# A graph network on one core: the scatter of left-over sums split by tile and set between the gathers

## The chip, the cores and the metric

The kernel runs on 1 core of a Trainium2 chip. Its time is the device time of one execution in microseconds. The kernel before was run three times: 4803.33, 4816.18 and 4818.72 us, median 4816.18. One further execution was recorded by the hardware profiler; the profile and all rows below are of that one.

## The reference

The program is four layers of a message passing network (PNA) over 6250 nodes with 64 features and 206,250 directed edges. In a layer each node takes, over its incoming edges, the sum, the mean, the greatest, the least, the variance and the standard deviation of the messages:

```python
msg = jnp.concatenate([h[src], h[dst]], axis=1) @ WM + bM
s = jax.ops.segment_sum(msg, dst, num_segments=n)
mean_sq = jax.ops.segment_sum(msg * msg, dst, num_segments=n) / denom
mx = jax.ops.segment_max(msg, dst, num_segments=n)
mn = jax.ops.segment_min(msg, dst, num_segments=n)
agg = jnp.concatenate([mean, mx, mn, std, var, s], axis=1)
hu = jnp.concatenate([h, agg, agg * amp, agg * att], axis=1) @ WU + bU
out = leaky_relu(batchnorm(hu / sqrt(n)) @ Wmix + bmix) + h
h = relu(batchnorm(out)) + h
```

The part of a message that comes from the source, `h[src] @ WM[:64]`, is a row of a table with one row per node (64 values, and their 64 squares). The part that comes from the target is the same for all edges of a node and is added afterwards. So what has to be gathered are rows of the table.

## The kernel before, in words

Before the four layers the kernel sorts the edges of each node. It puts at most one edge per node and block of 125 source nodes into a one-hot matrix (the dense part), and lists the edges that are left over (the second and further edges of a node from one block) in up to 64 columns. The nodes are ordered by how many left-over edges they have and stand in 50 tiles of 128 (`RT = TILES = 50`).

A layer has two parts.

The **dense part** (VectorE: `dense_part`, TensorE: `chunk`) runs over 13 chunks (`NCH`) of 482 nodes (`CH`), and in each over 50 steps, one per block: 650 steps a layer. A step is three matmuls at L1638 into one of five PSUM banks (`RING`), whose result VectorE folds into a running maximum (`greatest`, L1271; for the first two steps of a chunk a copy, L1269), and three matmuls at L1645 that sum up in one bank through the chunk, which ScalarE copies out at its end (L565). The matmuls of a step wait for VectorE to have read the bank (`g_used`); VectorE waits for `g_ready`, which TensorE raises with the third matmul. The one-hot matrix comes from DRAM on SyncE's queue (L448), five steps at a time, five such loads ahead; in layer 0 VectorE makes it (`compare`, L1287) from loaded node numbers (`RE<-vd`) and SyncE stores it.

Beside it, GpSimd fetches the **left-over rows**. `COL_GROUPS` is a fixed list of 166 groups. A group is one column of one to three neighbouring tiles, 457 such columns (`STATIC`) in all, each fetched by one indirect DMA of 128 rows (L808, a gather) into one of five ring places (`RING_G`). Before a group GpSimd waits for two things: that the group five before it has been added up (`joined`), and that the dense part has come within 12 steps (`AHEAD`) of the step at which the group is due (`g_ready`). The due steps are spread evenly from step 56 to step 580 (`COL_SPAN`). VectorE works a group in between the maxima, in three parts (L1324 and L1325 greatest and least, L1328 mask, L1333 add), into the sums `acc3` of 256 values per node in `accL`.

The first tiles have the most columns: tile 0 has 29, tile 1 has 17, tile 49 has 2. The list takes column 0 of all tiles, then column 1 and so on, with the single ones of tile 0 spread over it, so high tiles get their last column early and low tiles late.

When the last group is added up, GpSimd **scatters** the sums, which lie in the order of left-over edges, to the DRAM tensor `left` in the order of the nodes: 50 indirect DMAs of 128 rows of 1 KB (L836), one per tile. It waits until all have landed (`lf_sc`) and loads them back with ten plain DMAs (L841), which the second part of the layer reads. Two branches ahead of the scatter are for graphs that need more columns than planned: `rest` and `more`, which both are read at run time.

The **node part** (`node_part`) takes the dense results and the loaded left-over sums together (L1449 and on), multiplies by `WU` and `Wmix`, and normalizes.

What sets the order of the work is each engine's own program: the engines meet only at semaphores. GpSimd's program is written out in full for one layer (all 166 groups) in a loop over four.

## Time and profile before

| what | value |
|---|---|
| median of three runs | 4816.18 us |
| span of the profiled execution | 4821.6 us |
| mean granted clock of TensorE | 0.935 of full speed |
| TensorE busy | 3895.8 us (81%), 19240 matmuls |
| VectorE busy | 3426.7 us (71%) |
| GpSimd busy | 2229.1 us (46%) |
| ScalarE busy | 508.7 us (11%) |

The profile gives no other time of that execution than its span, from the first to the last instruction. Its first 390 us are the sorting of the edges; then come four layers of about 1100 us. Layers 1 to 3 are alike: layer 1's maxima run from 1532 to 2453 us, and GpSimd's gathers from 1582 to 2308 us; the scatters follow at 2319 us, and the node part at 2456 us. Layer 0 carries the making of the one-hot matrix too.

Times in the rows are microseconds from the start of the span, durations of single instructions in ns where marked so. PE is TensorE, DVE VectorE, ACT ScalarE, POOL GpSimd, SP SyncE. A busy time on GpSimd for a DMA is the time in which it makes the descriptors, not the transfer.

### The profile page before, as it was taken

How to read it: one execution, taken by the hardware profiler on the slowest of the kernel's cores; microseconds unless marked ns; L12 is line 12 of the kernel's file. 1: busy time of each engine (PE TensorE's matmuls, PEld its weight loads, DVE VectorE, ACT ScalarE, POOL GpSimd, SP SyncE). 2: the span in 40 equal slices, each digit the busy share in tenths (PEclk: the TensorE clock that was granted, in tenths of full speed). 3: DMA queues.
4: the chain of work that ended last, by engine and by line, in shares of the span. 5: the costliest groups of instructions: out<-in, count | busy, mean ns of one | idle time of the engine just before them, and what ended most of it. 6: DMA issues, size and time to landing. Idle time of an engine off the chain costs nothing.

```text
span 4821.6 us, 69713 instructions
## 1 busy us (share of the span) xinstructions
PE 3895.8 (81%) x19240; PEld 2004.6 (42%) x19240; DVE 3426.7 (71%) x7809; ACT 508.7 (11%) x1496; POOL 2229.1 (46%) x2241
## 2 busy tenths in 40 slices
PE   0165999998688999999587999999597999899586
PEld 0022444443265444444265444444265444444255
DVE  5795888898477777777377777777367677777466
ACT  4211000000034000000034000000024000000024
POOL 6204566666500566666500556666500466666600
PEclk9987999999799999999799999999799999999898
DMA  6005888888741444444531444444441444444450
GB/s 176 9 16 146 223 228 217 229 234 212 208 155 58 139 137 136 139 136 136 155 117 55 136 132 127 146 135 131 140 151 40 130 137 140 134 136 131 133 171 28
DMA packets 302954, 667.77 MB, mean 138 GB/s; under 512 B 82191, under 2 KB 180677, under 8 KB 302435
## 3 DMA queue, kind: packets, MB, share of 16 engines
q1 hardware_dynamic: 188676, 419.32, 29.7%
q0 software_dynamic: 81280, 191.65, 15.3%
q10 hardware_dynamic: 32732, 54.15, 3.4%
q14 instruction: 208, 1.70, 0.1%
q8 instruction: 58, 0.95, 0.1%
HBM read 517.17 MB, written 151.72 MB: 139 GB/s over the span
## 4 chain that ended last, share of the span: by engine, by line
PE 58%; another core or an unknown queue 19%; DVE 10%; issue 6%; ACT 2%; POOL 2%; DMA 1%; ACTq 1%; DVEq 0%; SPq 0%; POOLq 0%
PE bank L1638 27%; PE bank L1645 24%; PE bank L1722 3%; DVE scr L1271 2%; POOL accL L766 1%; PE bank L1710 1%; DVE RE L1082 1%; POOL accL L758 1%; DVE accL L1038 1%; DMA RE<-vd 1%; DVE accL L1039 1%; PE bank L1620 1%; PE bank L1694 0%; ACT scr L690 0%
## 5 line engine op out<-in xcount | busy, mean ns | idle before, releaser
L808 POOL DMA_INDIRECT rows<-table,lists x1828 | 1832.8, 1003 | 1269.8 <-issue 645.0
L1638 PE MATMUL bank<-RE,split 126*128 126x482 bf16 x7800 | 2061.8, 374 | 346.5 <-DVE scr L1271 268.4
L1271 DVE TENSOR_TENSOR scr<-scr,bank 128x482 f32<-128x482 f32 x2496 | 1594.6, 649 | 1026.5 <-PE bank L1638 615.0
L1645 PE MATMUL bank<-RE,split 125*128 125x482 bf16 x7800 | 2058.5, 373 | 143.1 <-ACT scr L565 122.7
L1638 PEld LDWEIGHTS bank<-RE,split 126*128 126x128 bf16 x7800 | 749.8, 98 | 1272.9 <-DVE scr L1271 348.5
L1645 PEld LDWEIGHTS bank<-RE,split 125*128 125x128 bf16 x7800 | 766.8, 98 | 1016.1 <-ACT scr L565 128.9
L565 ACT COPY scr<-bank 128x482 f32<-128x482 f32 x52 | 29.1, 560 | 3704.9 <-PE bank L1645 1772.1
L1333 DVE TENSOR_TENSOR accL<-accL,rows 128x384 f32<-128x384 f32 (+2 forms) x664 | 342.8, 516 | 0.0
L1328 DVE SCALAR_TENSOR_TENSOR rows<-CNT,rows 128x384 f32<-128x384 f32 (+2 forms) x664 | 342.6, 516 | 0.0
L793 POOL MEMSET accL<- 128x3328 f32 x4 | 11.5, 2871 | 682.5 <-DVE split L1260 681.5
L836 POOL DMA_INDIRECT left<-accL,lists x200 | 195.6, 978 | 110.5 <-issue 110.5
L1324 DVE TENSOR_TENSOR accL<-accL,rows 128x192 f32<-128x192 f32 (+2 forms) x664 | 221.0, 333 | 1.7 <-issue 1.0
L1325 DVE TENSOR_TENSOR accL<-accL,rows 128x192 f32<-128x192 f32 (+2 forms) x664 | 220.7, 332 | 0.0
L1722 PE MATMUL bank<-W,rows 128*125 128x192 f32 x624 | 126.5, 340 | 39.8 <-ACT scr L690 39.8
L772 POOL DMA_INDIRECT pos_d<-accL,nid x50 | 50.1, 1002 | 230.5 <-DVE nid L1163 215.5
L1287 DVE TENSOR_SCALAR RE<-RE,col 126x2410 bf16<-126x2410 bf16 x130 | 113.2, 871 | 28.2 <-DMA RE<-vd 26.5
L1722 PE MATMUL bank<-W,RE 128*125 128x192 f32 x576 | 113.1, 332 | 20.2 <-ACT scr L690 19.3
L1722 PEld LDWEIGHTS bank<-W,rows 128*125 128x125 f32 x624 | 101.8, 193 | 47.9 <-issue 38.1
L1269 DVE COPY scr<-bank 128x482 f32<-128x482 f32 x104 | 67.0, 655 | 59.3 <-remote 28.4
L1722 PEld LDWEIGHTS bank<-W,RE 128*125 128x125 f32 x576 | 90.7, 187 | 28.0 <-issue 25.1
L1449 DVE TENSOR_TENSOR rows<-bank,accL 125x256 f32<-125x256 f32 x100 | 42.6, 426 | 77.8 <-PE bank L1698 76.1
L1710 PE MATMUL bank<-ident,aggb 125*128 125x125 f32 x600 | 83.4, 276 | 4.8 <-DVE aggb L1469 4.8
(272 smaller groups left out, 2370.6 us busy)
## 6 DMA issues: line engine op xcount, KB each, us to landing
RE<-ohd SPq DMA_DIRECT2D x395, 593.1 KB
RE<-vd SPq DMA_DIRECT2D x130, 593.1 KB
ohd<-RE SPq DMA_DIRECT2D x130, 593.1 KB
rows<-table,lists POOLq DMA_INDIRECT x1828
dense_d<-scr ACTq DMA_DIRECT2D x104, 241.0 KB
accL<-left POOLq DMA_DIRECT2D x40, 625.0 KB, 19.3
split<-dense_d ACTq DMA_DIRECT2D x16, 750.0 KB, 8.6
table<-accL SPq DMA_DIRECT2D x36, 250.0 KB
```

The source lines that it names most:

```text
L808: nc.gpsimd.indirect_dma_start(ring[:, b * GC + k, :], None, table, bass.IndirectOffsetOnAxis(ap=lists[:, c:c + 1], axis=0)).then_inc(col_ ...
L836: nc.gpsimd.indirect_dma_start(left, bass.IndirectOffsetOnAxis(ap=lists[:, t * PAY + D:t * PAY + D + 1], axis=0), acc3[:, t, :], None).the ...
L1271: nc.vector.tensor_tensor(accM[k % 2], accM[k % 2], G[k % RING][:, 0:CH], ALU.max).then_inc(S["g_used"], 1)
L1287: nc.vector.tensor_scalar(BK[b][0:NP + 1, :], VB[g % 2][0:NP + 1, :], answers[0:NP + 1, :], None, ALU.is_equal).then_inc(S["cmp"], 1)
L1324: nc.vector.tensor_tensor(acc[:, :, 2 * D:3 * D], acc[:, :, 2 * D:3 * D], got[:, :, 0:D], ALU.max)
L1325: nc.vector.tensor_tensor(acc[:, :, 3 * D:4 * D], acc[:, :, 3 * D:4 * D], got[:, :, 0:D], ALU.min).then_inc(S["tops"], 1)
L1328: nc.vector.scalar_tensor_tensor(got, bcast(CNT[:, t:t + w].unsqueeze(2), [P, w, 2 * D]), float(r), got, ALU.is_gt, ALU.mult).then_inc(S[" ...
L1333: nc.vector.tensor_tensor(acc[:, :, 0:2 * D], acc[:, :, 0:2 * D], got, ALU.add).then_inc(S["joined"], 1)
L1638: ins = nc.tensor.matmul(G[k % RING][:, 0:CH], split[0:NP + 1, ORDER[k], q, 0:2 * D], columns_of(k, NP + 1), start=q == 0, stop=q == 2)
L1645: ins = nc.tensor.matmul(SB[:, 0:CH], split[0:NP, ORDER[k], q, D:3 * D], columns_of(k, NP), start=k == 0 and q == 0, stop=k == TILES - 1 a ...
L1710: ins = nc.tensor.transpose(FPS[(2 * j + a) % 3][:, c * NP:(c + 1) * NP], agg[j % 2][0:NP, a, 2 * c:2 * c + 2, :], id125)
L1722: nc.tensor.matmul(u, aggT[j % 2][a][:, c * NP:(c + 1) * NP], W[:, W_U + c * 192:W_U + (c + 1) * 192], start=a == 0 and c == 0, stop=False ...
```

## The change

Each tile's scatter is issued as soon as five groups (`RING_G`) have gone by since its last group, so that the `joined` wait ahead of the group vouches that its sums are complete. Behind the gathers of a group at most one tile is scattered. A tile under 25 (`HALF`) waits for `acc_ready` first, the semaphore by which ScalarE tells that it has cleared these sums. What is left after the last group is scattered at the end as before. In the two branches for larger graphs the whole scatter is done again with semaphores of its own, and VectorE waits there for the first one before it changes the sums.

```diff
+LAST_GROUP = [max((g for g, (_, t0, w) in enumerate(COL_GROUPS) if t0 <= t < t0 + w), default=-1) for t in range(RT)]
...
+                def scatter(t, signal):
+
+                    nc.gpsimd.indirect_dma_start(left, bass.IndirectOffsetOnAxis(ap=lists[:, t * PAY + D:t * PAY + D + 1], axis=0),
+                                                 acc3[:, t, :], None).then_inc(S[signal], 16)
+
+                to_scatter = sorted(range(RT), key=lambda t: LAST_GROUP[t])
                 for g, (r, t, w) in enumerate(COL_GROUPS):
...
+                    done = [t for t in to_scatter if LAST_GROUP[t] + RING_G <= g][:1]
+                    for t in done:
+                        if t < HALF:
+                            wait(pool, "acc_ready", l * 3 + 3)
+                        scatter(t, "lf_sc")
+                        to_scatter.remove(t)
                 wait(pool, "joined", (l + 1) * NG + RING_G)
+                for t in to_scatter:
+                    scatter(t, "lf_sc")
                 with pool.If(rest > 0):
...
+                    for t in range(RT):
+                        scatter(t, "lf_rest")
+                    wait(pool, "lf_rest", (l + 1) * (16 * RT))
                 with pool.If(more > 0):
...
-                    pool.sem_inc(S["passed"])
-
-                for t in range(RT):
-                    nc.gpsimd.indirect_dma_start(left, bass.IndirectOffsetOnAxis(ap=lists[:, t * PAY + D:t * PAY + D + 1], axis=0),
-                                                 acc3[:, t, :], None).then_inc(S["lf_sc"], 16)
+                    for t in range(RT):
+                        scatter(t, "lf_more")
+                    wait(pool, "lf_more", (l + 1) * (16 * RT))
+
                 wait(pool, "lf_sc", (l + 1) * (16 * RT))
...
             def further_rounds(l):
 
+                wait(dve, "lf_sc", (l + 1) * (16 * RT))
...
                     wait(dve, "joined", (l + 1) * NG + RING_G)
+                    wait(dve, "lf_sc", (l + 1) * (16 * RT))
```

By the list 44 of the 50 tiles find a group, and 6 remain for the end. The due steps of the groups behind which a scatter stands, in runs of neighbouring groups: 192 and 195; 303 to 310 (3 scatters); 359 to 366 (3); 403 to 420 (6); 445 to 456 (4); 480 to 497 (6); 511 to 527 (6); 538 to 552 (5); 558 to 580 (9).

GpSimd's program at the layer's end, before: the last three groups of gathers, and behind the branches the whole scatter in a row. L364 are the registers and waits.

```order
L808 DMA rows<-table,lists 128x128 [waits g_ready]
L808 DMA rows<-table,lists 128x128 x2
L364 REGISTER_ALU
L364 REGISTER_ALU [waits joined]
L808 DMA rows<-table,lists 128x128 [waits g_ready]
L808 DMA rows<-table,lists 128x128
L364 ISA
L811 COMPARE_AND_BRANCH [waits joined]
...
L836 DMA left<-accL,lists 6400x256 x50
L364 REGISTER_ALU
L841 DMA accL<-left 125x1280 [waits lf_sc]
L841 DMA accL<-left 125x1280 x9
```

The same place now: L818 are the gathers, L807 the scatters, L861 the loads.

```order
L818 DMA rows<-table,lists 128x128 [waits g_ready]
L818 DMA rows<-table,lists 128x128 x2
L807 DMA left<-accL,lists 6400x256 [waits acc_ready]
L367 REGISTER_ALU
L367 REGISTER_ALU [waits joined]
L818 DMA rows<-table,lists 128x128 [waits g_ready]
L818 DMA rows<-table,lists 128x128
L807 DMA left<-accL,lists 6400x256 [waits acc_ready]
L367 ISA
L807 DMA left<-accL,lists 6400x256 [waits joined]
L807 DMA left<-accL,lists 6400x256 x5
```

Six of the fifty scatters are left in the row; each group in front of it has one of its own.

In the stretch of groups due at steps 480 to 497, before:

```order
L808 DMA rows<-table,lists 128x128 x2
L364 REGISTER_ALU
L364 REGISTER_ALU [waits joined]
L808 DMA rows<-table,lists 128x128 [waits g_ready]
L808 DMA rows<-table,lists 128x128 x2
```

and now:

```order
L818 DMA rows<-table,lists 128x128 x2
L807 DMA left<-accL,lists 6400x256 [waits acc_ready]
L367 REGISTER_ALU
L367 REGISTER_ALU [waits joined]
L818 DMA rows<-table,lists 128x128 [waits g_ready]
L818 DMA rows<-table,lists 128x128 x2
L807 DMA left<-accL,lists 6400x256 [waits acc_ready]
```

A group of three gathers has become three gathers and a scatter.

## Rows read from the trace of the kernel before

**Rows 1.** The page's costliest groups: busy us, mean ns | idle before.

```profile
L808 POOL DMA_INDIRECT rows<-table,lists x1828 | 1832.8, 1003 | 1269.8 <-issue 645.0
...
L836 POOL DMA_INDIRECT left<-accL,lists x200 | 195.6, 978 | 110.5 <-issue 110.5
```

**Rows 2.** Windows of layer 1: from:to, length, busy us of each engine.

```profile
core 0: us, PE busy (x) PEld busy (x) DVE busy (x) ACT busy (x) POOL busy (x), PEclk, DMA share, GB/s
...
1596.00:2181.00 585.00, 537.51 (x2549) 246.75 (x2547) 435.04 (x958) 4.48 (x8) 365.60 (x371) 0.97 0.48 137
2181.00:2318.00 137.00, 131.08 (x615) 60.24 (x614) 108.84 (x245) 1.12 (x2) 78.28 (x80) 0.96 0.48 138
2318.00:2394.00 76.00, 27.63 (x113) 11.14 (x112) 12.58 (x20) 0.56 (x1) 53.95 (x60) 0.65 0.43 134
2394.00:2454.00 60.00, 59.41 (x287) 27.81 (x285) 31.60 (x49) 0.37 (x1) 0.00 (x0) 0.98 0.83 244
```

**Rows 3.** Timeline of VectorE: start, us busy, line, [idle before <-releaser].

```profile
2326.42 0.66 DVE L1271 TENSOR_TENSOR scr<-scr,bank 128x482 f32<-128x482 f32 x1 [0.57 <-DVE scr L1271]
...
2342.15 0.66 DVE L1271 TENSOR_TENSOR scr<-scr,bank 128x482 f32<-128x482 f32 x1 [5.68 <-remote]
2355.49 0.66 DVE L1271 TENSOR_TENSOR scr<-scr,bank 128x482 f32<-128x482 f32 x1 [12.68 <-remote]
2371.59 0.66 DVE L1271 TENSOR_TENSOR scr<-scr,bank 128x482 f32<-128x482 f32 x1 [15.45 <-remote]
...
2400.30 0.66 DVE L1271 TENSOR_TENSOR scr<-scr,bank 128x482 f32<-128x482 f32 x1 [0.57 <-PE bank L1638]
2401.53 0.66 DVE L1271 TENSOR_TENSOR scr<-scr,bank 128x482 f32<-128x482 f32 x1 [0.56 <-PE bank L1638]
```

**Rows 4.** Timeline of GpSimd, layer 1: first and last scatter of 50, first loads.

```profile
2319.42 1.00 POOL L836 DMA_INDIRECT left<-accL,lists  x1 [10.89 <-issue]
...
2382.06 0.97 POOL L836 DMA_INDIRECT left<-accL,lists  x1 [0.30 <-issue]
2385.08 5.26 POOL L841 DMA_DIRECT2D accL<-left  x10 [2.04 <-DMA left<-accL,lists]
```

**Rows 5.** Timeline of TensorE in the row of scatters.

```profile
2334.09 0.77 PE L1638 MATMUL bank<-RE,split 126*128 126x482 bf16 x3
...
2356.20 1.39 PE L1638 MATMUL bank<-RE,split 126*128 126x482 bf16 x3 [10.74 <-DVE scr L1271]
```

**Rows 6.** Timeline of GpSimd: a row of 9 gathers, a row of 12.

```profile
2112.48 0.98 POOL L808 DMA_INDIRECT rows<-table,lists  x1 [2.73 <-PE bank L1638]
...
2122.52 0.95 POOL L808 DMA_INDIRECT rows<-table,lists  x1 [0.30 <-issue]
2127.47 0.95 POOL L808 DMA_INDIRECT rows<-table,lists  x1 [4.00 <-PE bank L1638]
...
2161.62 0.98 POOL L808 DMA_INDIRECT rows<-table,lists  x1 [1.16 <-PE bank L1638]
...
2175.66 0.95 POOL L808 DMA_INDIRECT rows<-table,lists  x1 [0.31 <-issue]
2179.49 1.01 POOL L808 DMA_INDIRECT rows<-table,lists  x1 [2.88 <-remote]
```

**Rows 7.** Timeline of VectorE: the last late wait beside each of these rows.

```profile
2125.40 0.66 DVE L1271 TENSOR_TENSOR scr<-scr,bank 128x482 f32<-128x482 f32 x1 [1.48 <-PE bank L1638]
...
2178.76 0.66 DVE L1271 TENSOR_TENSOR scr<-scr,bank 128x482 f32<-128x482 f32 x1 [4.65 <-remote]
```

**Rows 8.** Windows, L1271 alone: from:to, length, VectorE busy (count), PEclk, DMA.

```profile
1234.00:1311.00 77.00, 13.98 (x23) 0.69 0.58 178
...
1596.00:2181.00 585.00, 260.03 (x407) 0.97 0.48 137
...
2318.00:2394.00 76.00, 10.70 (x17) 0.65 0.43 134
```

**Rows 9.** Timeline of VectorE in layer 0, behind the scatters.

```profile
1335.50 0.85 DVE L1287 TENSOR_SCALAR RE<-RE,col 126x2410 bf16<-126x2410 bf16 x1 [20.54 <-DMA RE<-vd]
```

**Rows 10.** The loads at L841 in layer 1 (2384 to 2460 us).

```profile
DMA to landing us min/median/max: 5.5/19.8/44.5
```

More of the change, by code:

```diff
@@ L339, in build @@
             "kb_done big_v big_ready big_next big_found big_rows big_added big_reset "
-            "gathered listed own_done paid idx_ready summed added tops masked joined lf_sc "
+            "gathered listed own_done paid idx_ready summed added tops masked joined lf_sc lf_rest lf_more "
             "t_ps t_used mq_ready sq_done x_ready agg_a agg_v at_ps at_ev u_ps scaled hu_done ht_ps hut_ev fin_v shift "
```

## The prediction

> **What bounds the kernel now.** The profiled execution has a span of 4821.6 us, 5.4 us (0.1%) above the median of the three runs, 4816.18. I read first the costliest groups of the page: GpSimd issues 1828 gathers and 200 scatters, that is 457 and 50 in each of four layers [rows 1]. Then the busy times by stretch, to see what TensorE does meanwhile. A layer's dense part is 650 steps. A step is three matmuls at L1638, three at L1645 and one maximum on VectorE (L1271; L1269 for two of the fifty in a chunk). With GpSimd silent TensorE is busy for 59.4 of 60 us [rows 2] and a step takes 1.23 us (the last two of [rows 3]): there the matmuls bound it. Beside the gathers TensorE is busy for 537.5 of 585 us, and in the 76 us in which the scatters run for only 27.6 [rows 2]. So the scatter row, though it is on an engine that nobody seems to need just then, is the worst stretch of the layer.
>
> The timeline of VectorE shows how. In the row of scatters, from 2319.4 to 2383.0 us [rows 4], VectorE has its usual waits until 2326.4; then one maximum waits 5.7 us, the next 12.7, the next 15.5 [rows 3]. TensorE had issued matmuls at L1638 five banks ahead, the last at 2334.09, and then waited for VectorE, so it is TensorE's signal that comes late; the signal back takes effect within 0.1 us of the maximum's end (2355.49 + 0.66, matmul at 2356.20 [rows 5]). The first six scatters do no harm and the others nearly stop the two engines. Gathers do the same in small: after 9 in a row GpSimd pauses 4.0 us and VectorE's late wait is 1.5 us; in a row of 12 that wait is 4.7 us [rows 6, 7]. I take it that what hurts is GpSimd issuing without a pause, of either kind, from about the seventh DMA on. The trace doesn't say why.
>
> **What goes.** In layer 1 the window 2318 to 2394 holds 17 maxima at L1271 and 2 copies at L1269, 19 steps [rows 8]; at 1.23 us they need 23.4 us, so 52.6 of 76 us are lost. Layers 2 and 3 show the same 17 in 76 us each. In layer 0 the window 1234 to 1311 holds 23 and 2, so 30.8 us of work in 77: 46.2 lost. Behind it VectorE waits 20.5 us for a load of node numbers [rows 9], which stays. In the changed kernel six scatters are left at the end, after a wait for the last sums. Six is as many as did no harm. So up to 3 x 52.6 + 46.2 = 204 us go.
>
> What comes next there is not late: the six scatters take 6 x 1.28 = 7.7 us, their landing 2.0 (GpSimd's wait before the loads of the sums [rows 4]), the loads at most 44.5 us (median 19.8) after issue [rows 10]: some 55 us after the last sum, and 66 steps at 1.23 us, 81 us, are left of the dense part. The loads already ran beside full-speed matmuls at 1.23 us a step, so I take nothing for them.
>
> **What comes.** 44 scatters a layer go between the gathers, 176 in all, each at the end of a group. By the plan's table 5 stand near steps 190 to 310, 13 from 359 to 456, and 26 from step 480 to 580, there behind nearly every group. The added wait for the cleared sums (tiles under 25) was met hundreds of steps before. The other two added waits are in branches that this graph doesn't take (the trace has no instruction of them), and cost nothing.
>
> A group of three gathers comes every 524/457 x 3 = 3.44 steps, 4.23 us at TensorE's own pace. GpSimd needs 3 x 1.255 = 3.77 us for it, and with a scatter 5.04. (1.255 is the distance of two gathers in a row, 1.278 of two scatters [rows 4, 6].) Before, GpSimd could run ahead to its limit (12 steps, or five groups) and pause, and in the pause TensorE's signals got through. With a scatter behind each group it is slower than TensorE, so it pauses only when TensorE stalls. The price of a scatter between gathers is not in the trace. Bounds from rows:
> - 0 us, if it fits into the pauses: in 2181 to 2318 us GpSimd issues 80 gathers, 100.4 us, and is idle for 36.6; 26 scatters take 33.2.
> - 0.8 us: 5.04 - 4.23, GpSimd never pausing.
> - 1.2 us: the same, with the 2.9 us pause of the row of twelve behind every 12 to 15 DMAs, 0.2 us on each of the four: 5.04 + 0.9 = 5.9 us a group, against 4.75 now, 3.44 steps of 1.38 us (407 maxima and 17 copies in 585 us [rows 8]).
> - 1.62 us, if GpSimd gets no larger share of the time than now: in 585 us, 371 gathers, 465.6 us, 79.6% [rows 2]; 1.28 / 0.79.
> - 2 us and more, if the gathers also come late.
>
> I take 1.4 us, between the last two: for the pause between rows is not spare time, it ends when TensorE's signal arrives; and the longer rows of DMAs lie just where 26 of the scatters go. That makes 176 x 1.4 = 246 us, against 204 gone: **+42 us**. On the profiled execution 4864, on the median **4858 us**. The two break even at 204 / 176 = 1.16 us.
>
> The Trainium skill speaks against a cost at all: its page "SBUF — State Buffer", section "Who interferes with whom", says "DMA never contends with a compute engine", so a scatter beside matmuls would cost GpSimd's time alone. By that rule the price would be 0, the first bound. The trace doesn't side with it, since TensorE is busy 27.6 of 76 us beside a row of nothing but DMAs [rows 2]; the rule is about ports, though, and a late signal may be another thing.
>
> **The rivals.**
> 1. *The pauses take them.* Price 0 to 1.08 us; at 0 all 204 us are gained, 4612 us; at 0.6, 98 us, 4718. For it: the 36.6 us of idle time; a late signal reaches TensorE only after five PSUM banks are full, some 6 us; the earlier 18 scatters are sparse. Against: rows of 12 already cost TensorE time, and 100.4 + 33.2 of 137 us leaves 3.4 us of pauses.
> 2. *GpSimd falls behind.* Its lead of 12 steps, 14.8 us, is used up by 26 scatters that exceed TensorE's pace by 0.8 us each, 21 us; then VectorE waits for gathered rows, which it now never does. Price 2 us: 352 - 204 = +148, 4964 us. It decides where the lead is gone before step 580. Against: stalls of TensorE give the lead back.
> 3. *The stall isn't the row's.* If a chunk's end (it falls into the row) or the loads behind it were the cause, the 204 us stay, and the scatters cost GpSimd only idle time: 4816. Against: 1596 to 2181 us holds chunk ends too, with TensorE busy for 92%, and the loads are issued at 2385, behind the stall [rows 4].
>
> **Numbers.** Three executions lie within 0.3% of each other, so 0.3%, 14 us, is what counts as a difference. Forecast, price over 1.24 us: 0.55. Price 1.08 to 1.24, with rival 3: 0.14. Rival 1: 0.27. Rival 2: 0.04. So slower 0.59, same 0.14, faster 0.27. The forecast alone has 4830 to 4897 (1.24 to 1.62 us). For 8 in 10 the range goes down to a price of 0.75 us, 4744, and up to 1.66, 4904.
>
> **What would show it.** Right: VectorE's waits of 5 to 16 us beside a row of scatters are gone, and what lies behind the gathers takes some 82 us instead of 136 (76 + 60 [rows 2]) in layers 1 to 3. If they don't, the first part is wrong. The window of steps 480 to 580, now about 137 us, grows by 26 x 1.4 = 36 us, with GpSimd's rows of DMAs longer than 12 there and waits of VectorE for TensorE's signal of over 5 us. If it grows by under 20 us, rival 1 has it; if VectorE's maxima on gathered rows (L1324) come to wait for a DMA, rival 2. Steps 56 to 359 should move by less than 10 us a layer. The forecast is wrong in sign if the gather stretch grows by less than 47 us a layer on average.

## The result, and the profile after

The changed kernel takes 4847 us (median of 15 runs, 4820 to 4882), against 4821 us for the kernel before on the same chip (15 runs, 4796 to 4844). The ratio is 1.0049 with an interval of 1.0025 to 1.0073: it is slower by 12 to 35 us, 24 in the middle (0.5%). Single executions of one kernel lie up to 1.3% apart, so it takes the 15 of each to see this. The profiled execution has a span of 4859.9 us, 38.3 more than that of before; it was 14.5 us above its own median, so the two traces show the same change somewhat enlarged.

I compare equal work: a stretch runs from the first record of one step to that of another, a step being one maximum (or one of the two copies of a chunk) on VectorE. The scatters between gathers all lie in steps 56 to 583, the row of 50, or what is left of it, in 583 to 649. In us, layers 0 to 3:

| steps | before | after | sum of the differences |
|---|---|---|---|
| 56 to 359 | 422.7, 418.9, 425.5, 422.9 | 432.2, 433.3, 429.6, 424.2 | +29.3 |
| 359 to 480 | 159.5, 168.0, 164.6, 163.7 | 183.1, 180.5, 188.8, 189.6 | +86.2 |
| 480 to 583 | 146.5, 135.4, 140.9, 140.6 | 177.9, 173.8, 169.8, 176.8 | +134.9 |
| 583 to 649 | 145.8, 135.0, 135.0, 134.9 | 94.0, 80.8, 79.2, 80.8 | -215.9 |
| all else (steps 0 to 56, nodes, start) | | | +3.8 |

So 250.4 us came and 215.9 went. The costliest groups after, the counterparts of [rows 1], and the maxima and the adders of the gathered rows (busy, mean ns | idle before, what ended it):

```profile
L818 POOL DMA_INDIRECT rows<-table,lists x1828 | 1827.3, 1000 | 1282.9 <-issue 646.0
...
L1292 DVE TENSOR_TENSOR scr<-scr,bank 128x482 f32<-128x482 f32 x2496 | 1600.4, 652 | 1056.7 <-PE bank L1660 632.0
...
L807 POOL DMA_INDIRECT left<-accL,lists x200 | 207.8, 1039 | 115.8 <-DVE accL L1355 57.3
L1346 DVE TENSOR_TENSOR accL<-accL,rows 128x192 f32<-128x192 f32 (+2 forms) x664 | 222.5, 335 | 0.9 <-DMA rows<-table,lists 0.9
```

The counts are the same; a scatter takes 1039 ns in place of 978, 12 us in all. The last row, L1346, is L1324 of the kernel before: VectorE waits 0.9 us there in the whole kernel for gathered rows.

Windows of layer 1 of before at the bounds of steps 56, 480, 583 and 649 (from:to, length, busy us and count of PE, PEld, DVE, ACT, POOL, then PEclk, DMA share, GB/s):

```profile
1595.60:2317.90 722.30, 668.89 (x3164) 307.16 (x3162) 544.18 (x1202) 5.61 (x10) 444.09 (x450) 0.97 0.48 137
2317.90:2452.90 135.00, 86.63 (x398) 38.93 (x396) 43.55 (x68) 0.56 (x1) 53.95 (x60) 0.80 0.61 184
2182.50:2317.90 135.40, 129.48 (x610) 59.62 (x609) 107.24 (x243) 1.12 (x2) 77.09 (x79) 0.97 0.47 136
```

and the same work after, the counterpart of [rows 2] too:

```profile
1613.30:2400.90 787.60, 690.19 (x3163) 311.12 (x3161) 548.00 (x1202) 5.60 (x10) 486.03 (x494) 0.93 0.46 133
2400.90:2481.70 80.80, 80.80 (x398) 38.33 (x396) 43.66 (x67) 0.56 (x1) 11.09 (x16) 1.00 0.82 236
2227.10:2400.90 173.80, 140.76 (x614) 61.59 (x613) 108.17 (x242) 1.12 (x2) 103.88 (x105) 0.88 0.43 127
```

TensorE is busy all of the 80.8 us behind the gathers, where before it was busy for 86.63 of 135.0 with the same 398 matmuls: 48.4 us of waiting and 5.8 us of lower clock are gone. In steps 480 to 583 it stands still for 33.0 us in place of 5.9, and the same matmuls take 11.3 us more at a granted clock of 0.88. GpSimd issues 79 gathers there before and 26 scatters more after. It is not busier than it was: 79 x 1.255 of 135.4 us leaves it 36 us idle, 79 x 1.255 + 26 x 1.278 of 173.8 leaves 41. The scatters fitted into none of its idle time.

GpSimd at the end of layer 1, the counterpart of [rows 4] (start, busy, line, idle before):

```profile
2384.59 0.99 POOL L807 DMA_INDIRECT left<-accL,lists  x1 [0.30 <-issue]
2401.59 0.98 POOL L807 DMA_INDIRECT left<-accL,lists  x1 [16.02 <-DVE accL L1355]
...
2407.98 0.97 POOL L807 DMA_INDIRECT left<-accL,lists  x1 [0.30 <-issue]
2411.00 5.26 POOL L861 DMA_DIRECT2D accL<-left  x10 [2.05 <-DMA left<-accL,lists]
```

and VectorE, the counterpart of [rows 3] and [rows 7], in the gather stretch and behind it (`remote` stands where the profile finds no instruction that gave the signal at that time):

```profile
2252.47 0.66 DVE L1292 TENSOR_TENSOR scr<-scr,bank 128x482 f32<-128x482 f32 x1 [4.51 <-remote]
...
2330.08 0.66 DVE L1292 TENSOR_TENSOR scr<-scr,bank 128x482 f32<-128x482 f32 x1 [5.13 <-remote]
...
2407.13 0.66 DVE L1292 TENSOR_TENSOR scr<-scr,bank 128x482 f32<-128x482 f32 x1 [0.54 <-DVE scr L1292]
2408.35 0.66 DVE L1292 TENSOR_TENSOR scr<-scr,bank 128x482 f32<-128x482 f32 x1 [0.57 <-issue]
```

The six left scatters run beside usual waits; the long waits have gone, and waits of 4 to 5 us, as [rows 7] has once, now come oftener beside the gathers: in steps 480 to 583 of the four layers 18 maxima wait over 4 us, where before 4 did, and the longest waits 6.6 us in place of 4.9. GpSimd's longest unbroken row in layer 1 was 13 DMAs before and is 21 now. The loads land after

```profile
DMA to landing us min/median/max: 6.1/22.5/45.8
```

against [rows 10], so they are not late. Steps 583 to 649 of layer 0 stay longer (94.0 us) because VectorE's waits for node numbers (`RE<-vd`) stay there: 36.0 us of them.

### The profile page after: what moved, and what is told of

Same layout as the page of the kernel before. It is cut to its first block, busy times and chain, and to the rows that moved or that the text cites. A ratio compares the mean times of both kernels' runs of the same rounds, so it can differ in the third digit from the quotient of the medians.

```text
span 4859.9 us, 69789 instructions
## 1 busy us (share of the span) xinstructions
PE 3965.6 (82%) x19240; PEld 2016.8 (41%) x19240; DVE 3440.3 (71%) x7809; ACT 513.4 (11%) x1496; POOL 2233.5 (46%) x2241
## 4 chain that ended last, share of the span: by engine, by line
PE 57%; another core or an unknown queue 19%; DVE 11%; issue 7%; ACT 3%; DMA 2%; ACTq 1%; DVEq 0%; POOL 0%; SPq 0%
PE bank L1660 27%; PE bank L1667 24%; PE bank L1744 3%; DVE scr L1292 2%; DMA RE<-vd 1%; PE bank L1732 1%; DVE RE L1102 1%; DMA accL<-in_dst,scr 1%; DVE accL L1058 1%; DVE accL L1059 1%; PE bank L1642 1%; ACT scr L693 1%; DVE accL L1355 0%; ACT rows L683 0%
## 5 line engine op out<-in xcount | busy, mean ns | idle before, releaser
L818 POOL DMA_INDIRECT rows<-table,lists x1828 | 1827.3, 1000 | 1282.9 <-issue 646.0
L1660 PE MATMUL bank<-RE,split 126*128 126x482 bf16 x7800 | 2095.8, 379 | 367.7 <-DVE scr L1292 283.4
L1667 PE MATMUL bank<-RE,split 125*128 125x482 bf16 x7800 | 2093.6, 378 | 87.2 <-ACT scr L568 62.0
L807 POOL DMA_INDIRECT left<-accL,lists x200 | 207.8, 1039 | 115.8 <-DVE accL L1355 57.3
L1346 DVE TENSOR_TENSOR accL<-accL,rows 128x192 f32<-128x192 f32 (+2 forms) x664 | 222.5, 335 | 0.9 <-DMA rows<-table,lists 0.9
```

The source lines that it names most:

```text
L807: nc.gpsimd.indirect_dma_start(left, bass.IndirectOffsetOnAxis(ap=lists[:, t * PAY + D:t * PAY + D + 1], axis=0), acc3[:, t, :], None).the ...
L818: nc.gpsimd.indirect_dma_start(ring[:, b * GC + k, :], None, table, bass.IndirectOffsetOnAxis(ap=lists[:, c:c + 1], axis=0)).then_inc(col_ ...
L1346: nc.vector.tensor_tensor(acc[:, :, 2 * D:3 * D], acc[:, :, 2 * D:3 * D], got[:, :, 0:D], ALU.max)
L1660: ins = nc.tensor.matmul(G[k % RING][:, 0:CH], split[0:NP + 1, ORDER[k], q, 0:2 * D], columns_of(k, NP + 1), start=q == 0, stop=q == 2)
L1667: ins = nc.tensor.matmul(SB[:, 0:CH], split[0:NP, ORDER[k], q, D:3 * D], columns_of(k, NP), start=k == 0 and q == 0, stop=k == TILES - 1 a ...
```

## The experiments

The theory as it stood: TensorE's signals come late when GpSimd issues indirect DMAs without a pause; a pause cures it, and a scatter beside gathers costs because it takes the pauses away. The rivals: it is the traffic or the scatters' landing; it is the place (the chunk's end, the loads). Later a second question came: is it the length of the unbroken row, or the mean rate? Each run is compared with runs of the kernel before on its own chip (medians 4821 to 4872); stretches from different chips can differ by 2%.

**1. Waiting for the landings.** In the row of before:

```diff
                 for t in range(RT):
+                    if t and t % 6 == 0:
+                        wait(pool, "lf_sc", l * (16 * RT) + 16 * t)
```

> The kernel before, with one wait added in the row of 50 scatters: after every 6 GpSimd waits until they have landed. Theory A (TensorE's signals are held up once GpSimd has issued about seven indirect DMAs without a pause, and get through in a pause): the 5 to 16 us waits of VectorE beside the row are gone, steps 583 to 649 take 81 to 90 us instead of 135 in layers 1 to 3, about 52 us gained there; the row takes 50 x 1.28 + 8 x 2.6 = 85 us instead of 64, so the loads come some 20 us later and the node part may wait up to 12 us for the first. In all 4 x (-50 + 5 to 12), a gain of 150 to 180 us (3 to 4%). Theory B (the stores to DRAM themselves, 6.4 MB in scattered rows, hold the signals up): the same stores go out in 85 us, so the stall stays for the most part, 0 to 15 us gained a layer, or some lost. Theory C (the stall is due to something else at that place): nothing gained, up to 20 us a layer lost by later loads.

Measured: 4768.88 against 4870.3 us, ratio 0.9795 (0.977 to 0.982). Steps 583 to 649 take 83.6, 80.0, 80.4 and 81.2 us: the same 50 scatters in the same place, and nothing is left of the stall. The gain is 101 us where 150 to 180 were expected, for the waits for the landing take 2 to 7 us each:

```profile
2326.42 0.97 POOL L838 DMA_INDIRECT left<-accL,lists  x1 [0.30 <-issue]
2331.03 0.97 POOL L838 DMA_INDIRECT left<-accL,lists  x1 [3.63 <-DMA left<-accL,lists]
...
2343.46 0.97 POOL L838 DMA_INDIRECT left<-accL,lists  x1 [5.07 <-DMA left<-accL,lists]
...
2357.78 0.97 POOL L838 DMA_INDIRECT left<-accL,lists  x1 [6.95 <-DMA left<-accL,lists]
```

so the row lasts 98 us, the loads start later, and the part of the nodes behind them takes 188 to 199 us a layer, where it takes 152 to 173 in run 3 on the same chip. The place is not the cause; landing or rate stay open.

**2. At most two under way.** The same with two semaphores in turn (the scatter then raises `side`, and the end waits for both):

```diff
+                    side = ("lf_sc", "lf_b")[t % 2]
+                    if t >= 2:
+                        wait(pool, side, l * (8 * RT) + 16 * (t // 2))
...
```

> The kernel before, with every scatter of the row waiting until the one two before it has landed, so that no more than two are under way. A scatter takes 1.0 us to issue and lands some 2 us later, so one goes out about every 1.5 to 1.7 us, with short pauses of 0.5 to 0.7 us in place of the 0.3 us. Theory A in the form that GpSimd's share of busy time counts: the stall shrinks to less than half, since GpSimd is busy 60 to 65% of the row and not 76%. Theory A in the form that an unbroken row counts and only a pause of 2 us or more ends it: the stall stays at 50 us a layer or gets longer with the row. Theory B: the stall stays.

Measured: 4846.06 against 4870.3, ratio 0.9957 (0.9941 to 0.9973). Steps 583 to 649 are free (77.6 to 80.8), but a scatter comes only every 2.39 us (1.5 to 1.7 were expected), and the nodes' part takes 212 to 222 us in place of 152 to 173. A pause need not be long, and should not hang on the landings.

**3. Gathers in the scatters' place.** The row reads from the table into the sums, then one plain store writes them; the placing of the sums by node is left out.

```diff
-                    nc.gpsimd.indirect_dma_start(left, bass.IndirectOffsetOnAxis(ap=lists[:, t * PAY + D:t * PAY + D + 1], axis=0),
-                                                 acc3[:, t, :], None).then_inc(S["lf_sc"], 16)
+                    nc.gpsimd.indirect_dma_start(acc3[:, t, 0:2 * D], None, table,
+                                                 bass.IndirectOffsetOnAxis(ap=lists[:, t * PAY:t * PAY + 1], axis=0)).then_inc(S["lf_sc"], 16)
...
```

> The kernel before, but its row of 50 scatters is a row of 50 gathers (table rows into the sums, which are so overwritten), and one plain DMA then stores all sums to DRAM: the output is not the reference's, what is left out is the placing of the sums. Theory A: the row of gathers stalls TensorE as the row of scatters does: VectorE's waits grow to 10 us and more beside it, TensorE is busy less than half of it. Theory B: no stall beside the gathers, as nothing is stored then, and one beside the plain store behind them.

Measured: one time, 4891.63 us. Steps 583 to 649: 164.4, 135.4, 136.0, 134.2, where the 50 scatters had 135. In VectorE's timeline:

```profile
2393.59 0.66 DVE L1273 TENSOR_TENSOR scr<-scr,bank 128x482 f32<-128x482 f32 x1 [5.70 <-remote]
2406.88 0.66 DVE L1273 TENSOR_TENSOR scr<-scr,bank 128x482 f32<-128x482 f32 x1 [12.64 <-remote]
2423.69 0.66 DVE L1273 TENSOR_TENSOR scr<-scr,bank 128x482 f32<-128x482 f32 x1 [16.15 <-remote]
2441.18 0.66 DVE L1273 TENSOR_TENSOR scr<-scr,bank 128x482 f32<-128x482 f32 x1 [16.83 <-remote]
```

That is [rows 3] over again with 5.70, 12.64, 16.15: the direction is without effect, and so is the size of a row, which is 512 bytes here and 1 KB in the scatters. Nothing is stored to DRAM by the row. The gathers come every 1.25 us, a little closer, and the last waits are a little longer.

**4. The same bytes in one plain DMA.** One transfer in place of the row; the order of the nodes is left out.

```diff
-                for t in range(RT):
-                    nc.gpsimd.indirect_dma_start(left, bass.IndirectOffsetOnAxis(ap=lists[:, t * PAY + D:t * PAY + D + 1], axis=0),
-                                                 acc3[:, t, :], None).then_inc(S["lf_sc"], 16)
...
+                nc.gpsimd.dma_start(left.rearrange("(p i) f -> p i f", i=RT), acc3[:, 0:RT, :]).then_inc(S["lf_sc"], 16)
...
```

> The kernel before with one plain DMA of the same 6.4 MB in place of the row of 50 scatters (each partition's sums in one piece, so in the wrong order: the output is not the reference's). Theory A: no stall, steps 583 to 649 take about 81 us in layers 1 to 3; a span some 200 us shorter. Theory B: the stores hold up TensorE's signals as before, for 20 us and more.

Measured: one time, 4680.66 us; windows of layer 1, steps 583 to 649, of run 3 and of this one:

```profile
2371.80:2507.10 135.30, 89.25 (x398) 39.19 (x396) 43.46 (x67) 0.56 (x1) 52.93 (x61) 0.79 0.63 191
```

```profile
2326.50:2407.10 80.60, 80.60 (x397) 38.27 (x396) 43.82 (x68) 0.56 (x1) 5.77 (x11) 1.00 0.96 291
```

More bytes a second than in any other window printed here, 291 GB/s at a DMA share of 0.96, and TensorE never waits in layers 1 to 3. (In layer 0 the stretch takes 110.9 us; VectorE's long waits there are for the loads of node numbers, 42.2 us, not for TensorE.) It is not the bytes; it takes the indirect DMAs. Whether what hurts is GpSimd's issuing or the 128 single rows that each of them moves was not separated: no run moves such rows without GpSimd.

**5 and 6. A pause that waits for nothing outside.** A clearing of an unused buffer after every sixth scatter of the row, two of them (5) or one (6). The cut is that of run 6; run 5 has `range(2)` and 16 in place of 8:

```diff
+                def pause():
+
+                    pauses[0] += 1
+                    nc.gpsimd.memset(pad[:, 0:750], 0.0).then_inc(S["paused"], 1)
+                    wait(pool, "paused", l * 8 + pauses[0])
...
+                    if t and t % 6 == 0:
+                        for _ in range(1):
+                            pause()
```

> The kernel before, but after every 6 of the row's 50 scatters GpSimd clears a scratch tile of 128x750 twice and waits for it (some 0.7 us each by the memsets of the first kernel, with the semaphores about 2 us), in place of the wait for the landing in the run with paced scatters, whose pauses came out at 2.2 to 7 us. Theory A (an unbroken row of DMA issues holds TensorE's signals, a short pause frees them): no stall, steps 583 to 649 take 80 to 82 us, the row takes 64 + 8 x 2 = 80 us instead of the 98 measured with landings, the loads start 18 us earlier, and the node part takes 170 to 175 us instead of 191: 4 x 45 us faster than before, 3.7%. Theory D (TensorE's signals get through only when the scatters have landed, so that nothing is under way): the stall stays for the most part, 30 us and more a layer.

> The same with one clearing each, about 1 us of pause: the row takes 64 + 8 x 1 = 72 us. Theory A says nothing of how short a pause may be. If 1 us is enough, steps 583 to 649 take 80 to 84 us and the node part 165 to 167: 4 x 52 us faster than before, 4.3%. If the backlog of a row of six needs longer to drain, waits of VectorE of 2 us and more show behind the third or fourth group of six, and steps 583 to 649 take 90 to 120 us.

Measured: 4650.95 (ratio 0.9639, 0.9594 to 0.9684) and 4631.23 (0.9597, 0.9555 to 0.9639) against 4826.8 us. With one clearing steps 583 to 649 take 87.9, 80.8, 80.8 and 80.8. GpSimd's timeline around one clearing, and the window of steps 583 to 649 in layer 1:

```profile
2276.59 0.97 POOL L848 DMA_INDIRECT left<-accL,lists  x1 [0.30 <-issue]
2277.56 0.74 POOL L807 MEMSET pad<- 128x750 f32 x1
2279.09 0.98 POOL L848 DMA_INDIRECT left<-accL,lists  x1 [0.79 <-issue]
```

```profile
2268.80:2349.60 80.80, 80.80 (x398) 38.33 (x396) 42.91 (x67) 0.56 (x1) 55.32 (x60) 1.00 0.67 228
```

The clearing and its semaphore put 1.23 us more between two DMAs; eight of them, 10 us a layer, buy back 54.

**7. A pause beside the gathers too.** As 6 with two clearings in the row, and one ahead of every second group of gathers:

```diff
+                    if g % 2 == 0:
+                        for _ in range(1):
+                            pause()
```

> The run with two clearings in the row, and besides one clearing (about 1 us) ahead of every second group of gathers, so that no row of gathers is longer than six, in all 83 us of pauses a layer. Theory A: TensorE's signals aren't held up, a step beside the gathers takes 1.23 to 1.28 us instead of 1.38, steps 56 to 583 take 645 to 675 us instead of 727: 50 to 80 us gained a layer on top of row6_pad2. Against it: the pauses add to GpSimd's work, 6 gathers and a clearing are 8.5 us against 8.4 us for TensorE's 6.9 steps. Theory E (GpSimd's share of the time counts, not its rows): the pauses only replace waits that it has now, and steps 56 to 583 stay at 720 to 740 us. If GpSimd is too slow with them, VectorE waits for gathered rows at L1324 and they take over 740 us.

Measured: 4611.86 against 4826.8, ratio 0.9566 (0.9518 to 0.9615). Steps 56 to 583: 735.9, 710.5, 710.8, 709.6, where 645 to 675 were expected if the pauses cure the signals' lateness and cost nothing else. Groups of the page:

```profile
L820 POOL DMA_INDIRECT rows<-table,lists x1828 | 1818.8, 995 | 984.4 <-issue 492.9
L1287 DVE TENSOR_TENSOR scr<-scr,bank 128x482 f32<-128x482 f32 x2496 | 1587.8, 648 | 244.7 <-PE bank L1654 161.6
L1340 DVE TENSOR_TENSOR accL<-accL,rows 128x192 f32<-128x192 f32 (+2 forms) x664 | 225.5, 340 | 554.5 <-DMA rows<-table,lists 510.3
```

The maxima's waits fell from 834.9 us (run 6) to 244.7, and the adders' rose from 2 to 554.5: the waits for TensorE's signals are mostly gone and GpSimd is too slow. It is what the prediction had as its second rival, here brought about by the pauses.

**8 and 9. Shorter pauses, more widely spaced.** A clearing of 128x300 ahead of every third group and after every sixth scatter (8), and one of 128x64 ahead of every second and after every sixth (9), one clearing each time. Run 9's against that of run 7:

```diff
-                    nc.gpsimd.memset(pad[:, 0:750], 0.0).then_inc(S["paused"], 1)
+                    nc.gpsimd.memset(pad[:, 0:64], 0.0).then_inc(S["paused"], 1)
```

> Pauses of one clearing of 128x300 (0.3 us; with the semaphore about 1.1 us, in the gathers 1.4) after every 6 scatters of the row and ahead of every third group of gathers, so rows of at most nine gathers. In the run with rows of six, GpSimd had become the bound: VectorE waited 510 us for gathered rows and only 245 for TensorE's signals (632 before). Nine gathers and a pause are 11.3 + 1.4 = 12.7 us against 12.6 for TensorE's 10.3 steps. Theory A with an onset at seven DMAs: two or three DMAs of each row are over it, waits of VectorE of up to 2 us, and a step takes 1.28 to 1.33 us, steps 56 to 583 675 to 705 us: some 10 to 35 us a layer less than with rows of six. If a pause of 1.1 us doesn't free the signals, a step takes 1.38 us or more and steps 583 to 649 over 100 us.

> Rows of six, each ended by a clearing of 128x64 (under 0.1 us; with the semaphore about 0.9 us, in the gathers 1.2, instead of the 0.3 us between two DMAs). Six gathers and a pause are 7.5 + 1.2 = 8.7 us, against 8.4 for TensorE and 9.4 in the run with the longer clearing. Theory A with pauses of 0.9 us being enough: a step beside the gathers takes 1.26 to 1.30 us, steps 56 to 583 take 665 to 690 us, and 583 to 649 81 us with a row of 50 x 1.28 + 8 x 0.6 = 69 us: the fastest so far, 4540 to 4590 us where before is 4820. If what frees the signals is GpSimd's idle time as such and 0.9 us per six is too little, steps 56 to 583 stay at 700 to 740 us and waits of 5 us and more show beside the row of scatters.

Measured: 4628.43 (ratio 0.959, 0.9557 to 0.9624) and 4629.22 (0.9622, 0.9579 to 0.9666) against 4824.94. Steps 56 to 583 take 703 to 717 us in run 8, 690 to 708 in run 9, the best of all; but the stall at the end comes back by half, 105 to 108 us and 117 to 120 us in layers 1 to 3, though no row of scatters is longer than six (81 us was expected of run 9, and a total of 4540 to 4590). So an unbroken row of more than six is not what decides.

**10. A pause after twelve.** As 6, but `t % 12 == 0`.

> As the run with one clearing of 128x750 after six scatters, but after twelve. Theory A with its onset at seven and the waits of the kernel before (5.7 us by the 18th scatter, 12.7 by the 28th): each row of twelve ends before VectorE's waits pass 3 to 4 us, and a pause of 1.5 us frees the signals; TensorE loses 2 to 4 us a row, so steps 583 to 649 take 88 to 97 us, between the 80.8 of rows of six and the 135 of one row of fifty. If a pause of 1.5 us can't drain a row of twelve, the rows add up and it is over 110 us.

Measured: one time, 4758.63 us; steps 583 to 649 take 105.6, 122.1, 121.8, 122.7 (88 to 97 were expected). The windows of layer 1 of run 10 and of run 9:

```profile
2295.10:2417.10 122.00, 89.91 (x397) 38.98 (x396) 43.16 (x68) 0.56 (x1) 56.97 (x64) 0.83 0.64 184
```

```profile
2240.90:2357.40 116.50, 92.49 (x386) 38.99 (x385) 43.49 (x69) 0.56 (x1) 55.59 (x68) 0.81 0.65 190
```

Set beside the mean distance between two of the row's DMAs, all runs fall into one order. Both columns are of layers 1 to 3; the last is the stretch less 80.8 us:

| run | DMAs in a row | mean distance us | lost in steps 583 to 649, us |
|---|---|---|---|
| 3, gathers | 50 | 1.25 | 53 to 55 |
| before | 50 | 1.28 | 54 |
| 10 | 12 | 1.38 | 41 to 42 |
| 9 | 6 | 1.39 | 36 to 39 |
| 8 | 6 | 1.42 | 24 to 27 |
| 6 | 6 | 1.48 | 0 |
| 11, below | 6 | 1.48 | 1 to 3 |
| 5, 1, 2 | 6, 6, 2 | 1.62, 1.9, 2.4 | 0 |

A pause after twelve and a shorter one after six give the same mean rate and nearly the same loss. It is as if something can take an indirect DMA of 128 rows in some 1.45 to 1.48 us, while GpSimd can issue one in 1.28. That is a reading of the table; no record in the trace shows the thing itself, and it holds for the row alone. Beside the gathers the mean distance is about 1.6 us in the kernel before, slower than the 1.48 that costs nothing in the row, and the stretch still takes 727 us in place of 648; there GpSimd issues in bursts at 1.25 us, with waits between.

Nor is it a plain queue, in which a signal stands behind the DMAs that have piled up. The trace of the kernel before shows when TensorE finished a bank and when VectorE could read it. The five banks that TensorE filled from 2329.19 to 2334.86 us ([rows 5] has the last) are read by the maxima at 2335.82, 2342.15, 2355.49, 2371.59 and 2387.69:

```profile
2329.19 0.78 PE L1638 MATMUL bank<-RE,split 126*128 126x482 bf16 x3
```

```profile
2328.73 0.66 DVE L1271 TENSOR_TENSOR scr<-scr,bank 128x482 f32<-128x482 f32 x1 [1.65 <-PE bank L1638]
2331.58 0.66 DVE L1271 TENSOR_TENSOR scr<-scr,bank 128x482 f32<-128x482 f32 x1 [2.19 <-PE bank L1638]
2335.82 0.66 DVE L1271 TENSOR_TENSOR scr<-scr,bank 128x482 f32<-128x482 f32 x1 [3.58 <-PE bank L1638]
...
2387.69 0.66 DVE L1271 TENSOR_TENSOR scr<-scr,bank 128x482 f32<-128x482 f32 x1 [15.44 <-remote]
```

So the first of the five comes 5.8 us after its matmuls have ended, the next 11.0, 23.1, 38.0, and the last 52.8 us after, behind the end of the row (2383.03). VectorE's waits of 5.7 to 15.5 us are only the distances between signals that are much later than that. Counted in the same way, in layer 1, the latest is 54.8 us late beside the row of run 3, 19.7 beside that of run 9 and 2.2 beside that of run 6. When the last bank was full, 12 scatters had been issued, and at 0.2 us too much each they would have piled up 2.4 us of work (an estimate from 1.28 and 1.48), not 53; and the last scatter of the row has landed 2.0 us after it was issued [rows 4]. While the row goes on, single signals get through, one in 6 to 16 us.

**11. Both.** `pause(64)` ahead of every second group and `pause(750)` after every sixth scatter.

> The pause that was best beside the gathers (a clearing of 128x64 ahead of every second group: steps 56 to 583 in 690 to 697 us) and the one that was best in the row (a clearing of 128x750 after six scatters: steps 583 to 649 in 80.8 us) in one kernel. The runs so far order by one number, the mean distance of DMAs in the row: 1.28 us costs 54 us, 1.38 41, 1.41 37, 1.45 25, 1.48 and more nothing. Theory F, which takes the place of the unbroken row: each of GpSimd's 128-row DMAs occupies something for about 1.47 us, TensorE's signals queue behind what is not yet done, and a pause helps only as far as it brings the mean distance to that. Then both gains add: about 4 x (30 + 54) less 4 x 5 for later loads, 4500 us where before is 4820, ratio 0.93 to 0.94. If one pause takes from the other (a third thing bounds the layer), it stays at 0.955 to 0.96.

Measured: 4582.21 us (five runs, 4571.8 to 4584.11) against 4872.42 (nine runs, 4848.6 to 4881.74), ratio 0.9406 (0.938 to 0.9432), the fastest of all. Steps 56 to 583 take 715 to 719 us, and on this chip runs 1 to 4, whose gathers are as before, have 732 to 747 (738.2 on the mean); steps 583 to 649 take 87.1, 82.3, 82.2 and 83.9. So the gains add, 290 us, though the one beside the gathers is 21 us a layer and not the 30 that was expected. Windows of both stretches in layer 1:

```profile
1535.50:2254.80 719.30, 663.97 (x3163) 303.50 (x3162) 546.52 (x1201) 5.76 (x11) 459.42 (x531) 0.99 0.47 138
2254.80:2337.10 82.30, 81.54 (x398) 37.94 (x396) 41.75 (x67) 0.56 (x1) 56.42 (x62) 1.00 0.67 225
```

**12. The changed kernel with each scatter between gathers doubled.** The second goes to a place that nobody reads:

```diff
                         scatter(t, "lf_sc")
+                        nc.gpsimd.indirect_dma_start(spare_d, bass.IndirectOffsetOnAxis(ap=lists[:, t * PAY + D:t * PAY + D + 1], axis=0),
+                                                     acc3[:, t, :], None).then_inc(S["lf_two"], 16)
...
```

> The changed kernel, with each of the 44 scatters a layer that stand between gathers issued twice, the second time into a DRAM tensor that nobody reads: 545 indirect DMAs from step 56 to 583 instead of 501 (457 in the first kernel). These take 1.58 us each in both kernels (727 / 457 and 790 / 501). Theory F: the stretch is bound by a fixed time per DMA, so it takes 545 x 1.58 = 860 us, 65 to 72 us a layer more, a span of 5120 to 5150 us, with no change behind step 583. The other theory, that a scatter fits in where there are pauses and costs only where they run out, has them all run out by now: the 18 early ones cost little in the changed kernel and more now, so the growth from 56 to 480 would be clearly larger than that of the first 18 (27 us a layer).

Measured: one time, 5141.15 us; steps 56 to 583 take 847.9, 861.0, 859.1 and 868.7 us. The stretch, on the mean of the four layers, over the indirect DMAs that belong to it (7 to 10 a layer are issued ahead of step 56):

| kernel | DMAs | us | us per DMA |
|---|---|---|---|
| before | 457 | 727.3 | 1.59 |
| after | 501 | 789.9 | 1.58 |
| gathers as before, on the doubled kernel's chip (runs 1 to 4) | 457 | 738.2 | 1.62 |
| doubled | 545 | 859.2 | 1.58 |

Steps 480 to 583 of layer 1 of the doubled kernel:

```profile
2328.70:2530.60 201.90, 145.78 (x620) 62.45 (x619) 108.14 (x242) 1.12 (x2) 128.28 (x126) 0.83 0.40 123
```

The doubled kernel's chip is 1% slower, 4872 us for before, and the expectation did not allow for that; that 860 us was hit is in part this. On its own chip the 88 scatters of a layer cost 859.2 - 738.2 = 121.0 us, 1.38 us each; the first 44 cost 1.42 (250.4 / 176), so about 1.33 is left for the second (121.0 - 62.6 over 44). The two spans say the same: 5141 - 4872 = 269 us, and 216 gained at the end, are 485 us for 352 scatters, 1.38 each. So twice as many scatters cost nearly twice as much, and nothing shows that they fit into idle time. The other theory expected steps 56 to 480 to grow by clearly more for the second 18 scatters than for the first, 28.9 us a layer. They grew by 42.7 over the changed kernel, of which some 10 are the chip (596.5 us with gathers as before in runs 1 to 4, 586.5 in the profile of before): 33, not clearly more.

Beside the gathers the stretch goes in the main at the pace of the indirect DMAs, not at TensorE's (527 steps at 1.23 us are 648). Not wholly: one more costs 1.3 to 1.4 us, less than the mean of 1.6. The pace is no fixed floor either, since run 9 with its pauses comes to 697.4 / 457 = 1.53.

## Why the prediction came out as it did

The forecast was 4858 us for a kernel that measures 4847 on one chip; its +42 us stands against +24 (12 to 35) by the runs and +38 by the profile. Slower had 0.59, and slower it is. The 14 us that were to count as a difference came from three executions; the 15 of before lie within 49 us, and three of each kernel might not have shown the sign. The small difference is that of two large terms, which came out 6% (what goes) and 2% (what comes) above the forecast.

- *The row nearly stops the two engines; up to 204 us go.* Right: 215.9 us went. The count of steps in a window that ended at 2394 left out the last us of each stall, 52.6 against 54.2 to 55.8 in layers 1 to 3, and 46.2 against 51.8 in layer 0. That it is the indirect DMAs and how densely they come, and not the place or the bytes, is shown by runs 1, 3, 4 and 6. The prediction read 5.7 us as the first late wait; those of 1.65, 2.19 and 3.58 us stand before it, so the lateness sets in by degrees, and it took the waits for the lateness, which is up to 52.8 us.
- *"From about the seventh DMA on", "GpSimd issuing without a pause".* This is the step that was wrong. Run 9 never has seven and loses 36 to 39 us a layer; what orders the runs is the mean distance. It did little harm to the number: the seventh DMA entered it as "six at the end do no harm", and a single row of six is harmless by either reading (80.8 us); and the pick of 1.4 us leaned on it in part. Nor does the mean distance explain the price beside the gathers, for in steps 480 to 583 of the changed kernel a DMA comes only every 1.63 to 1.73 us.
- *176 scatters at 1.4 us, +246.* Measured 250.4, 1.42 us each. By the runs' +24 in place of the profile's +38 it would be some 1.36. No row gave the 1.4: it was picked between 1.2 and 1.62 (which the text calls "the last two" of its bounds, though "2 us and more" is the last), and that it fell so near is in part luck. The picture of the 1.62, that GpSimd gets no larger share of the time, is nearest to what was found, with 1.42 and in run 12 1.38. The bound of 0.8 took TensorE's pace of 4.23 us a group as its floor, and that pace doesn't bound this stretch. The bound of 1.2 took too little pause: three gathers and a scatter at 1.67 us each are 6.7 us, not 5.9. By thirds of the stretch: steps 480 to 583 grew by 34 us on the mean (36 forecast), 359 to 480 by 21.6, 56 to 359 by 9.5, 14.4, 4.1 and 1.3 (below 10 forecast, missed in layer 1).
- *Six at the end do no harm, the loads are not late.* Right: 80.8 us against 82, and loads in 22.5 us at the median.
- *Rival 1, the pauses take them* (price 0 to 1.08). Fell. Its 36 us of idle time are still there, 41 of them, after 26 scatters more. Idle time that ends when a late signal arrives is not room for this work. The page "SBUF — State Buffer" of the Trainium skill, section "Who interferes with whom", says that DMA never contends with a compute engine. In runs 3 and 4 the plain transfer agrees with that, and beside the row of indirect ones TensorE loses time all the same: 6.55 MB (6400 x 256 x 4 bytes) in one go leave TensorE busy for 80.60 of 80.60 us, 50 gathers for 89.25 of 135.30. What it loses there are waits for signals, so the ports, of which the page speaks, are not shown to be in contention.
- *Rival 2, GpSimd falls behind.* Fell: 0.9 us of waits at L1346. Run 7 shows what it looks like when it is true, 554.5 us.
- *Rival 3, the stall isn't the row's.* Fell with the 80.8 us, and with run 1, which leaves the row in its place.

The break-even of 1.16 us a scatter becomes 215.9 / 176 = 1.23 by what was measured. Each of the 176 saves that much at the end and costs 1.42 beside the gathers.

What stays open: why TensorE's signals are late. The records show the lateness, between the end of TensorE's matmuls and VectorE's start, and the rate from which it begins in the row, and no more. Also open is what makes it set in beside the gathers at 1.6 us a DMA, the range between 1.42 and 1.48 us, and whether the limit is the same for DMAs of fewer rows or for such rows moved from another engine's queue, which weren't tried. Some of the loss is the clock and not the wait: in steps 56 to 583 of layer 1, 21.3 of the 65.3 us are busy time of the same matmuls at a granted clock of 0.93 in place of 0.97; a kernel that waits less gets this back with the rest (run 11: 0.99, and 663.97 us busy for the same matmuls).

## What to carry to other kernels

Count the indirect DMAs that GpSimd issues beside matmuls and divide the stretch by them: in this kernel that gave some 1.6 us, GpSimd's idle time was no room for more, and each one moved in cost 1.3 to 1.4 us. That the same figure means the same in another kernel is not shown. Look for VectorE waiting on a signal of TensorE while TensorE waits on VectorE, and on GpSimd issuing beside them. Where that is so, try first not to move the work; slow its issue a little, here by one small clearing after every six scatters, which gave 4%, and 6% with the gathers paced as well.

## What the runs showed of the hardware that was not expected

- GpSimd issues an indirect DMA of 128 rows every 1.25 us (gathers) or 1.28 us (scatters). In a row of 50 at that distance VectorE waits up to 16.8 us for one signal of TensorE, with one maximum between two such waits, and a signal arrives up to 54.8 us after the matmuls that raise it have ended; at a mean distance of 1.48 us neither happens, and between 1.38 and 1.42 the loss falls from 42 to 24 us in a row of 50.
- A clearing of 128x64 takes 0.17 us and one of 128x750 takes 0.74; between the DMAs around the larger there are 1.53 us instead of 0.30.
- A plain DMA of the same bytes, in a window at 291 GB/s and a DMA share of 0.96, leaves TensorE busy for 80.60 of 80.60 us in layer 1.
- Scatters set between gathers cost 1.42 us each (44 a layer) and 1.38 (88 a layer), though GpSimd shows 36 us of idle time in the 135 us where most of them go.
- One stall costs twice: TensorE's granted clock fell to 0.80 over the 135 us (0.65 in the 76 of the stall), and the same 398 matmuls took 86.63 us in place of 80.80.
